# Relation layer of a graph network on one core: basis sums added into SBUF rings, base products once per 128-node block

## What is computed

```python
x = layernorm(x + gnn0(x, edge_index, edge_weight, W1, b1, W2, b2))   # weighted mean of neighbours, two layers
# relation layer
hsrc = h[src]                            # h = x, a row for each edge
coef = w_comp[etype]                     # 32 relations x 8 bases
msg = sum(hsrc @ weight[b] * coef[:, b][:, None] for b in range(8)) * norm
node_repr = relu(segment_sum(msg, dst) + bias)
out = layernorm(x + node_repr)
```

## Time and profile before

| | us |
|---|---|
| median of 3 runs | 4108.58 |
| span of the profiled execution | 4082.7 |
| PE busy | 3569.6 (87%) |
| DVE busy | 2436.7 (60%) |
| POOL busy | 2280.6 (56%) |
| ACT busy | 1282.2 (31%) |

### The profile page before, as it was taken

How to read it: one execution, slowest core, us unless ns; L and a number is a source line. 1 busy time by engine, 2 the same in 40 slices (tenths; PEclk the granted TensorE clock), 3 DMA queues, 4 the chain that set the end, 5 groups by cost and what they waited for, 6 DMA issues and landing times.

```text
span 4082.7 us, 56981 instructions
## 1 busy us (share of the span) xinstructions
PE 3569.6 (87%) x17449; PEld 2412.3 (59%) x17449; DVE 2436.7 (60%) x4212; ACT 1282.2 (31%) x3177; POOL 2280.6 (56%) x2622
## 2 busy tenths in 40 slices
PE   3999999989999999999949888887889888898886
PEld 3899999965444444444426556565556555566555
DVE  7999999967876730220245556565556554555554
ACT  5999999950000000100012112221122111122121
POOL 6888888840045444444156556655556555555552
PEclk6999999999999999999968988988898888888886
DMA  6677777778799999999821112121221111212121
GB/s 186 192 206 206 208 206 209 204 249 285 243 272 283 269 270 283 272 284 290 255 54 51 52 51 59 52 54 51 54 53 52 52 53 51 56 48 55 53 54 32
DMA packets 492929, 603.14 MB, mean 148 GB/s; under 512 B 49454, under 2 KB 419168, under 8 KB 492528
## 3 DMA queue, kind: packets, MB, share of 16 engines
q1 hardware_dynamic: 439483, 508.97, 42.2%
q0 software_dynamic: 53136, 90.45, 8.6%
HBM read 430.82 MB, written 168.42 MB: 147 GB/s over the span
## 4 chain that ended last, share of the span: by engine, by line
PE 32%; SPq 21%; issue 17%; ACT 17%; DMA 6%; DVE 5%; DVEq 1%; POOL 1%; another core or an unknown queue 0%; ACTq 0%; POOLq 0%
PE PS L1089 20%; SPq L550 16%; ACT arena L725 11%; DMA arena<-adjacency 5%; ACT arena L741 5%; SPq L546 3%; PE PS L1156 3%; SPq L506 2%; PE PS L1196 2%; PE PS L976 1%; PE PS L1174 1%; DVE XT L1639 1%; PE PS L1187 1%; PE PS L1136 1%; DVE arena L1294 0%
## 5 line engine op out<-in xcount | busy, mean ns | idle before, releaser
L677 POOL DMA_INDIRECT arena<-x_table,rec x1208 | 1152.2, 954 | 909.3 <-issue 313.7
L976 PE MATMUL PS<-arena 128*98 128x128 f32 x6272 | 761.1, 278 | 47.2 <-ACT arena L741 12.1
L976 PEld LDWEIGHTS PS<-arena 128*98 128x98 f32 x6272 | 707.8, 166 | 96.8 <-issue 59.4
L660 POOL DMA_INDIRECT sorted_records<-arena x346 | 385.0, 1113 | 659.7 <-PE PS L1089 627.5
L619 POOL TENSOR_SCALAR arena<-iota,H,arena 128x98 f32<-128x98 f32 x980 | 673.7, 701 | 91.7 <-PE PS L976 89.0
L725 ACT ACTIVATE arena<-arena 128x98 f32<-128x98 f32 x1568 | 582.7, 686 | 13.6 <-DVE arena L1363 12.5
L1089 PE MATMUL PS<-arena,X 128*128 128x512 f32 (+1 forms) x1274 | 534.2, 574 | 26.3 <-DMA arena<-adjacency 25.9
L1089 PE MATMUL PS<-arena,H 128*128 128x512 f32 (+1 forms) x1274 | 530.4, 572 | 17.6 <-DMA arena<-adjacency 16.8
L1639 DVE TENSOR_TENSOR XT<-XT,PS 128x8 f32 (+1 forms) x1586 | 272.6, 172 | 436.2 <-PE PS L1196 148.7
L741 ACT ACTIVATE arena<-PS 98x1024 f32<-98x1024 f32 x392 | 519.4, 1325 | 11.8 <-PE PS L976 11.7
L1156 PE MATMUL PS<-H,X 128*128 128x512 bf16 x1274 | 463.6, 450 | 23.2 <-issue 22.9
(11 more groups left out here) (238 smaller groups left out, 2934.0 us busy)
## 6 DMA issues: line engine op xcount, KB each, us to landing
arena<-adjacency SPq DMA_DIRECT2D x294, 768.0 KB
adjacency<-arena SPq DMA_DIRECT2D x196, 784.0 KB
arena<-adjacency SPq DMA_DIRECT2D x98, 832.0 KB
arena<-x_table SPq DMA_DIRECT2D x1792, 0.5 KB
arena<-x_table,rec POOLq DMA_INDIRECT x1208
arena<-in_edge_type SPq DMA_DIRECT2D x279, 48.0 KB
arena<-in_edge_type SPq DMA_DIRECT2D x93, 64.0 KB
sorted_records<-arena POOLq DMA_INDIRECT x346
```

Source lines behind the costliest of these rows:

```text
L660: pool.indirect_dma_start(rec2_d, bass.IndirectOffsetOnAxis(ap=SLOT[:, t:t + 1], axis=0), R4[:, t, :], None).then_inc(s_scat, 16)
L677: pool.indirect_dma_start(G[:, n % 5 * UNIT_TILES + i, :], None, x1_d, bass.IndirectOffsetOnAxis(ap=SRC[:, t:t + 1], axis=0)).then_inc(s_g ...
L976: last = nc.tensor.matmul(bank(2 * q + j // 4, P, j % 4 * P)[0:M1, :], S1[:, r, :], S2[:, r, :], start=True, stop=True)
```

## The change

The base products leave the step. Two *rings* of basis sums stand in SBUF, each with room for 4 node blocks (`RING_BLOCKS`) and an overhang: `SUMS_G` for the gathered tiles (8 bases x 520 columns, in `XT`), `SUMS_S` for the sorted ones (8 x 554). DVE adds a unit's or a wide tile's sums straight out of PSUM into the ring, 8 x 8 or 8 x 42 elements at once, and ACT's copies L890 and L896 and `UB` are gone. When all tiles of a node block are added (an *event*: 39 blocks of the gathered ring, 12 of the sorted one, 51 in all), PE multiplies that block with the 8 bases (8 products of 128 columns), ACT rectifies it out of PSUM and writes zeros over the ring's block (43 times). Blocks 10 and 11 lie in both rings; their parts are kept and joined. An addition that runs into the overhang is folded back on wrapping (12 times).

With that: the seven comparisons of source numbers are one `tensor_scalar` of 512 columns each, reading an f16 copy in SBUF that ACT makes of the spread numbers (`rows_copied`). Groups go through the classes in turn (`group_of`). PSUM has four unit banks where it had three, and a bank is freed by DVE's additions. The residual is loaded from `x1_table` by SP. The row loads by SP are gone: POOL gathers all 13 tiles. `reprT`'s zeroing by DVE (L1644) is replaced by two memsets on POOL. The scatter of records begins at the same place and ends some 39 row blocks earlier. The checks of the input's layout are written anew.

```diff
-UNIT_BANKS = [0, 1, 6]
+UNIT_BANKS = [0, 1, 5, 6]
 def scatter_after(t):
-    return FIRST_SCATTER + min(t, ONE_EACH) + max(t - ONE_EACH, 0) * 3 // 4
+    return FIRST_SCATTER + t * 8 // 11
 # SP
-                        sp.dma_start(GS[at + i:at + i + 1, :], x1_d[bass.ds(node, 1), :]).then_inc(s_sprow[k % 2], 16)
+                sp.dma_start(in_blocks(HY2[m % 2], nb), rows(x1_d, at, nb)).then_inc(s_resid[m % 2], 16)
 # POOL
+            nc.gpsimd.memset(SUMS_G, 0.0).then_inc(s_zero, 1)
+            nc.gpsimd.memset(SUMS_S, 0.0).then_inc(s_zero, 1)
-                if by_sp(step, j):
-                    continue
 # ACT
+                nc.scalar.activation(SROW[i % 2], bank(3), ACT.Copy).then_inc(s_srowc, 1)
...
+            def block_taken(n):
+                step, ring, b = EVENTS[n]
+                act.wait_ge(s_bp, n + 1)
...
+                        nc.scalar.activation(to, product_at(), ACT.Relu, bias=bcol[:, 1:2]).then_inc(s_act, 1)
+                if reused(n):
...
+                    nc.scalar.activation(sums, zero[:, 0:1].unsqueeze(2).to_broadcast([P, BASES, width]), ACT.Copy).then_inc(s_freed, 1)
 # PE
-                for b in range(BASES):
-                    last = nc.tensor.matmul(bank(4 + s % 2, width), Wr[:, b, :], UB[s % 2][:, b, 0:width], start=(b == 0), stop=(b == BASES - 1))
-                last.then_inc(s_w, 1)
+            def block_multiplied(n):
+                step, ring, b = EVENTS[n]
+                pe.wait_ge(s_addg if ring == "gathered" else s_adds, added_after(step, ring))
...
+                for a in range(BASES):
+                    last = nc.tensor.matmul(product_at(), Wr[:, a, :], ring_block(ring, b)[:, a, :], start=(a == 0), stop=(a == BASES - 1))
+                last.then_inc(s_bp, 1)
+            def unit_bank_free(n):
+                if n >= 4:
+                    step, kind, i = UNITS[n - 4]
+                    if kind == "tile":
+                        pe.wait_ge(s_addg, added_tiles(step, i))
+                    elif kind == "wide":
+                        pe.wait_ge(s_adds, added_wide(step, i))
+                    else:
+                        pe.wait_ge(s_turned, step + 1)
 # DVE
-                for ks in (slice(0, 4), slice(4, CLASS_BLOCKS)):
-                    n = ks.stop - ks.start
-                    last = nc.vector.tensor_tensor(ST2[q % 2][:, ks, :], bank(3).unsqueeze(1).to_broadcast([P, n, PER * P]),
-                                                   NODE[:, ks].unsqueeze(2).to_broadcast([P, n, PER * P]), ALU.is_equal)
+                for k in range(CLASS_BLOCKS):
+                    last = nc.vector.tensor_scalar(ST2[i % 2][:, k, :], SROW[i % 2], NODE[:, k:k + 1], None, ALU.is_equal)
-                        nc.vector.tensor_tensor(a, a, bank(to, span, at), ALU.add).then_inc(s_add, 1)
+                a = SUMS_G[:, :, bass.ds(base, SPAN)]
+                nc.vector.tensor_tensor(a, a, bank(UNIT_BANKS[n % 4], BASIS, j * BASIS).rearrange("p (b j) -> p b j", j=SPAN), ALU.add).then_inc(s_addg, 1)
...
+                a = SUMS_S[:, :, bass.ds(base, WIDE)]
+                nc.vector.tensor_tensor(a, a, bank(UNIT_BANKS[n % 4], WIDE_BASIS).rearrange("p (b j) -> p b j", j=WIDE), ALU.add).then_inc(s_adds, 1)
...
+            for s in range(OUT_AT[-1] + 2):
+                if s < STEPS:
+                    for j, base in enumerate(tile_heads(s, 0)):
+                        tile_added(s, 0, j, base)
+                if s + 1 < STEPS:
+                    matrix(s + 1)
+                if s + 1 < GROUPS:
+                    wide_matrix(s + 1)
+                if s + 2 < GROUPS:
+                    sources(s + 2)
+                if s + 2 < STEPS:
+                    relations(s + 2)
...
+                if s < STEPS:
+                    rest_added(s)
```

More of the change, by code:

```diff
@@ new lines, in reused, with wraps, events_in, events_to @@
+def reused(n):
+    step, ring, b = EVENTS[n]
+    return b + RING_BLOCKS <= (NBLK - 1 if ring == "gathered" else LAST_S)
+def wraps(n):
+    step, ring, b = EVENTS[n]
+    return b % RING_BLOCKS == RING_BLOCKS - 1 and b < (NBLK - 1 if ring == "gathered" else LAST_S)
+def events_in(step):
+    return [n for n, event in enumerate(EVENTS) if event[0] == step]
+def events_to(step, what):
+    return len([n for n, event in enumerate(EVENTS) if event[0] <= step and what(n)])
+CHUNK_DONE = [max(EVENTS[n][0] for n in range(len(EVENTS)) if EVENTS[n][2] // OUT_BLOCKS == c) + 1 for c in range(len(OUT_CHUNKS))]
@@ L97 @@
 UNIT = {u: n for n, u in enumerate(UNITS)}
-UNIT_END = [max(n for n, u in enumerate(UNITS) if u[0] == step) + 1 for step in range(STEPS)]
 TYPED = -(-REGION // P)
@@ L180, in regular @@
         hc = sb("hc", [P, TBLK])
[L181 to L182 removed]
+        bad = sb("bad", [P, 13])
         WT_sb = sb("WT_sb", [P, 4, D])
@@ new lines, in tiles_summed @@
+            def tiles_summed(s, i):
+                n = UNIT[s, "tile", i]
+                unit_bank_free(n)
+                half = 2 * s + i
+                pe.wait_ge(s_c, half + 1)
+                pe.wait_ge(s_gath[half % HELD_UNITS], 16 * rows_until(half))
+                first, end = PARTS_OF_STEP[i]
+                for j in range(end - first):
+                    last = nc.tensor.matmul(bank(UNIT_BANKS[n % 4], BASIS, j * BASIS), G[:, half % HELD_UNITS * UNIT_TILES + j, :],
+                                            C[s % 2][:, first + j, :, :].rearrange("p b j -> p (b j)"), start=True, stop=True)
+                last.then_inc(s_u, 1)
@@ new lines, in heads_loaded, with tile_heads @@
+            def heads_loaded(values):
+                return nc.values_load_multi_w_load_instructions(
+                    values, engines=(mybir.EngineType.DVE,), min_val=0, max_val=RING_NODES - 1,
+                    skip_runtime_bounds_check_because="the table holds numbers masked to the ring's size")[1]
+            def tile_heads(s, i):
+                first, end = PARTS_OF_STEP[i]
+                return heads_loaded(table[0:1, REGION + s * STEP_TILES + first:REGION + s * STEP_TILES + end])
```

717 lines of the change are left out of this document (367 added, 350 removed).

## The result

The changed kernel took 4207.18 us (median of 4 runs, 4201.22 to 4228.37) against 4110.49 of the kernel before: ratio 1.024, 95% interval 1.0217 to 1.0262. Faster was forecast, it is slower. The span of the profiled execution is 4203.1 us, 120.4 more than before.

What follows compares the result with a forecast made beforehand. PE was taken to bound short steps and SP's row loads the long ones. Span 4082.7 - 170 - 167 - 14 = 3731.7 us, plus 25.9 to the runs' median: 3758 us, range 3655 to 3940.

Steps and rivals of the forecast that it cites:

- In a short step PE sets the time: Relation layer, kernel before: 16.1 us of PE work at clock 1.0 make a short step of 19.3 us.
- Term A: SP's row loads gone, POOL gathering instead: all steps fall from 21.13 to 19.3 us, 170 us gained.
- The long steps by SP: Relation layer: 21 steps take 23 to 30 us because SP's type loads come only behind 32 row loads.
- Term B: Work of a relation-layer step on PE and DVE: falls from 19.3 to 17.5 us, 167 us gained.
- the loop's 16.4: New loop in each step, PE and DVE waiting for each other: 16.4 us once round.
- Term C: Ends of the relation layer: 5 us less zeroing at the start, 9 us less at the end, 14 us gained.
- Late signals stay: PE's signals, 3.8 us late, now sit on the loop: 19.0 us a step, 3897 us; chance 0.23.
- Slower: Comparisons at 0.665 us each and every PE signal 3.8 us late: 22.5 us a step, 4225 us; chance 0.04.
- POOL is slowed by DVE: POOL's gathers stand still for DVE's comparisons, 2.4 us: POOL needs 18.7 us a step, 3870 us; chance 0.06.
- POOL's floor: POOL's 13 gathers, 16.3 us, bound the step at 16.5 us: 3665 us; chance 0.15.

Runs made afterwards that it cites:

- h2: Changed kernel, DVE's second-unit additions together, comparisons and normalization after them, POOL's gathers for both units given later waits: prompt chip 3666.63 us, ratio 0.9944.
- c1: Kernel before with no row loads by SP, POOL gathering all 13 tiles: prompt 3672.15 us (ratio 1.0004) and 3649.81 (0.9998), late 4186.64 (1.0163).

## Why the prediction was wrong

**"In a short step PE sets the time"** is the step that failed; the rest hangs on it. The short step of 19.4 us was PE's 16 us of work only by the busy share. On a late chip it is 13 gathers at 1.25 us from start to start, 16.25 us, in runs of 7 and 6, with two pauses of some 1.85 us in which PE's held signals arrive, 1.55 us more each than between two gathers: 19.35 us. The trace had it. POOL in the kernel before, around the L1590 that starts at 3618.69:

```profile
3608.45 0.94 POOL L677 DMA_INDIRECT arena<-x_table,rec  x1 [1.73 <-remote]
...
3615.93 0.94 POOL L677 DMA_INDIRECT arena<-x_table,rec  x1 [0.30 <-issue]
3618.76 0.94 POOL L677 DMA_INDIRECT arena<-x_table,rec  x1 [1.88 <-remote]
```

Seven gathers, an end at 3616.88, and 1.8 us later the coefficients, 3.8 us late, reach DVE, and another signal POOL. I took the lateness for a property of PE's stream and added it as slack.

**Term A** (170 us of gain) came out at +67 us on a late chip and 0 on a prompt one. The long steps by SP are real and went. "POOL takes the 14 tiles over ... which a 19.3 us step hides. I see nothing else that would be late there" is what failed: POOL's longer runs made other signals late. One reading was off as well: of the steps of which "21 take 23 to 30 us" one, the first step of all, takes 38.4, and gives 19 of the 164 us.

**Term B** (167 us of gain). Without held signals the step was 17.81 us for 17.5 forecast, and PE and DVE do wait for each other as described. That the number fits is partly luck: the 1.1 us added to the loop's 16.4 lean on the 3.2 us that the kernel before took above PE's work, and those the sum above gives to POOL; and a block's base products took 2.8 us in the mean (3.05 on the late chip) for 1.8, with DVE's wait for the second unit left out. The additions and comparisons were sized right. PE's upper bound of 17.6 us takes a third of its work at half clock; with the 0.86 of the earlier trace rows it would be 13.2 / 0.86 = 15.3. What was wrong above all is what the new step replaces: not 19.3 us of PE but 16.7, so on a prompt chip it is 93 x 1.12 = 104 us of loss (108 measured). On the late chip the change also moved PE's second unit and the next first one close together: they end 5.7 us apart (2980.45 and 2986.10), where L1174's ended 7.6 us apart (3606.11 and 3613.72). Six gathers take 7.2 us, so POOL now finds the next buffer free before it is through and runs of 13 form; this link is argued, no run moved the units alone. A and B together made +1.6 us a step, 149 us: 22.73 is the prompt chip's 17.81 and 4.9 us that came with held signals. The register loads L1713, which I put at 0.5 us a step, take 3 x 1.06; they mostly lie under PE's unit.

**Term C** (14 us). From the last matrix to DVE's last instruction it took 27.8 us for 38.9 (30 forecast). The layer also began 16.7 us earlier (2051.19 for 2067.92), but the kernel before began at 2052.9 in another run, so that part is no effect of the change. Sum: to the span's end 11.5 us less, and 4082.7 - 16.7 + 148.6 - 11.5 = 4203.1 us, the span.

**The rivals.** "Late signals stay" had the right place and too small a price: it took 3.8 us as given, and the change itself raised it to 10. "Slower" gave 4225 us, near the result, by another sum: the comparisons that it put at 0.665 us took 0.363, and held signals made 4.9 us a step where it had 3.8 and the comparisons' 2.3. The agreement is luck. "POOL is slowed by DVE" fell: a gather's mean is 951 ns (954 before), though seven `tensor_scalar` comparisons a step have come, and the 137 gathers that ran beside one took 949 ns. By the Trainium skill ("SBUF — State Buffer", section "SBUF: two separate sides") the comparisons should have held POOL's gathers up; no run here shows it. "POOL's floor" is what h2 reached on a prompt chip. The estimate from the Trainium skill ("VectorE: DVE Perf Modes", section "The perf-mode tier table"), 0.29 us a comparison, fits the distance from start to start (2.06 / 7), while one comparison is 0.363 us long.

## What to carry to other kernels

A wait put down to "remote" is a cause to be found, not slack to be kept: look at what every other engine does until the signal comes, POOL's gathers first, and whether the wait ends when that does. When work is moved to an engine that is busy two thirds of the time, ask how long its unbroken runs become, not only whether its sum fits. And time a tuned kernel and its change on more than one chip before a mechanism is read from one trace: the old kernel's short step was 19.4 us on one kind, set by POOL's gathers and pauses, and 16.7 on the other, set by PE (in c1's traces; with SP's rows it has the same time).

## What the runs showed of the hardware

On chips of the late kind PE's signals were held while POOL issued gathers back to back: those given 5 us or more into a run came up to 13 us late, most of them 1.5 to 2.7 us after the run's last gather, with PE issuing small matmuls only every 0.7 or 1.4 us meanwhile; on chips of the prompt kind 1222 gathers in one run held none (0.26 us). What does this, whether the recording has a part in it, and why only some chips show it, stays open. Nor did I expect that the row loads of SP, 30.6% of the chain in the earlier trace rows, are worth nothing on a prompt chip.
